# Output projection, second residual and second norm moved within steps 6 and 7 of a fused attention and recurrent kernel

## The reference, cut to what matters

```python
# x: 32 sequences of 256 rows of 128; 16 heads of 64, 4 persistent key/value rows per head
x = x + attention(layernorm(x))          # rms norm, qkv, rope on q and k, causal softmax, output projection
y = layernorm(x)                         # the second norm
# a recurrence over the 32 sequences, on a state c of 256 x 128 (shown for one step):
ft = sigmoid(xt @ wf.T + c @ uf.T + bf)
it = sigmoid(xt @ wi.T + c @ ui.T + bi)
gt = tanh(xt @ wc.T + c @ uc.T + bc)
c = ft * c + it * gt
# at the end
h = tanh(einsum('tbi,oi->tbo', y, wo) + c_final @ uo.T + bo)
x = x + h
```

## Time and profile before

| | |
|---|---|
| median of 3 runs | 1160.55 us (1159.35 to 1161.35) |
| the profiled execution, whole | 1162.89 us |
| its span in the trace | 1161.0 us |
| PE busy with matmuls | 1088.0 us, 94% of the span |
| PE weight loads | 826.2 us, 71% |
| DVE busy | 951.9 us, 82% |
| ACT busy | 707.2 us, 61% |
| POOL busy | 649.2 us, 56% |
| mean granted clock of PE | 0.976 of full speed |

### The profile page before, as it was taken

How to read it: one execution, slowest core, us unless ns; L and a number is a source line. 1 busy time by engine, 2 the same in 40 slices (tenths; PEclk the granted TensorE clock), 3 DMA queues, 4 the chain that set the end, 5 groups by cost and what they waited for, 6 DMA issues and landing times.

```text
span 1161.0 us, 47269 instructions
## 1 busy us (share of the span) xinstructions
PE 1088.0 (94%) x18411; PEld 826.2 (71%) x18411; DVE 951.9 (82%) x3304; ACT 707.2 (61%) x1603; POOL 649.2 (56%) x828
## 2 busy tenths in 40 slices
PE   4879999999999999999999999999999999999981
PEld 2557777777777777777777777777777777777671
DVE  6678888888878988888888888888888888888646
ACT  3556666666556566656666666666666566666634
POOL 3545555556555555655555565555646555655415
PEclk8799999999999999999999999999999999999995
DMA  6213333332333333233333323333332233333205
GB/s 204 93 71 99 112 112 112 112 112 77 96 110 107 113 112 99 90 98 112 105 112 113 110 86 93 110 112 113 112 112 90 85 108 108 108 107 107 72 2 145
DMA packets 78031, 120.52 MB, mean 104 GB/s; under 512 B 13041, under 2 KB 35954, under 8 KB 77682
## 3 DMA queue, kind: packets, MB, share of 16 engines
q1 hardware_dynamic: 68722, 111.21, 31.3%
q10 hardware_dynamic: 9088, 6.29, 2.0%
HBM read 41.56 MB, written 8.78 MB: 43 GB/s over the span
## 4 chain that ended last, share of the span: by engine, by line
PE 57%; DVE 15%; DMA 14%; SPq 5%; issue 4%; POOL 4%; ACT 2%; DVEq 0%; POOLq 0%; ACTq 0%
PE bank_pv L1081 10%; DMA rope_c<-rope_b 10%; PE bank L974 9%; PE bank_st L1037 7%; PE bank_sum L1118 6%; PE bank_sum L1102 4%; PE bank_sm L1013 4%; DMA linv_scratch<-linv 3%; DVE masked L781 3%; PE bank L996 3%; SPq L298 2%; DVE linv L804 2%; PE bank L993 2%; PE bank L1204 2%; PE bank L1206 2%
## 5 line engine op out<-in xcount | busy, mean ns | idle before, releaser
L396 POOL TENSOR_TENSOR qk<-rope_a,rope_c 128x512 f32<-128x512 f32 x256 | 340.7, 1331 | 304.8 <-DMA rope_c<-rope_b 300.8
L781 DVE CUSTOM_DVE_ANT_0 masked<-bank_sm,mask_q 128x132 bf16<-128x132 f32 (+1 forms) x1024 | 307.6, 356 | 44.2 <-PE bank_sm L1013 43.4
L389 POOL TENSOR_TENSOR prob<-prob 128x264 f32<-128x264 f32 x256 | 212.0, 828 | 157.6 <-ACT prob L535 150.7
L535 ACT ACTIVATE prob<-bank_st 128x784 f32<-128x784 f32 x256 | 210.3, 822 | 115.3 <-PE bank_st L1046 114.3
L770 DVE TENSOR_TENSOR rope_a<-bank,cos 128x512 f32<-128x512 f32 x256 | 174.3, 681 | 102.1 <-PE bank L974 74.6
L520 ACT ACTIVATE qk_h<-qk 128x512 f16<-128x512 f32 x256 | 160.2, 626 | 128.9 <-POOL qk L396 128.6
L1081 PE MATMUL bank_pv<-prob,v_sb 128*64 128x256 f32 (+1 forms) x2048 | 224.7, 340 | 0.6 <-DVE raw L797 0.6
L1037 PE MATMUL bank_st<-qk 64*64 64x196 f32 (+3 forms) x4096 | 185.7, 298 | 0.1
L771 DVE TENSOR_TENSOR rope_b<-bank,sin 128x512 f32<-128x512 f32 x256 | 173.8, 679 | 0.0
L1037 PEld LDWEIGHTS bank_st<-qk 64*64 64x64 f32 x4096 | 167.3, 133 | 9.0 <-issue 0.8
L1081 PEld LDWEIGHTS bank_pv<-prob,v_sb 128*64 128x64 f32 x2048 | 124.3, 136 | 54.3 <-issue 0.8
(11 more groups left out here) (202 smaller groups left out, 1793.7 us busy)
## 6 DMA issues: line engine op xcount, KB each, us to landing
rope_c<-rope_b SPq DMA_DIRECT2D x512, 128.0 KB, 2.1
rinv<-linv_scratch SPq DMA_DIRECT2D x124, 256.0 KB, 4.5
out<-x_sb SPq DMA_DIRECT2D x16, 256.0 KB, 2.5
linv_scratch<-linv SPq DMA_DIRECT2D x62, 64.0 KB, 2.1
x_sb<-x ACTq DMA_DIRECT2D x28, 128.0 KB, 5.3
pre<-w_qkv_t ACTq DMA_DIRECT2D x1, 1024.0 KB, 5.3
v_sb<-pm_v SPq DMA_DIRECT2D x64, 8.0 KB
v_end<-v_end_scratch SPq DMA_DIRECT2D x64, 8.0 KB
```

Of the source, the lines that this page charges most:

```text
L389: G.tensor_tensor(prob_2[:, s % 4, :, :], prob[:, s % 4, :, 0:NT - Q1], prob[:, s % 4, :, C0 + Q1:SCOL], ALU.add).then_inc(S["prob_added"], 1)
L396: G.tensor_tensor(qk[:, s, :].rearrange("p (u n) -> p u n", u=2)[:, :, 0:NT], rope_a[:, (NPAIR * j + s) % 3, :].rearrange("p (u n) -> p u ...
L535: A.activation(prob[:, s % 4, :, :], ps_st[:, :, 0:SCOL], ACT.Exp).then_inc(S["exp_done"], 1)
L781: ins = V.tensor_tensor_reduce(masked[:, e, c0:c0 + n], ps_sm[:, e, c0:c0 + n], mask_q[:, c0:c0 + n], 1.0, LOWEST, ALU.add, ALU.max, top[: ...
```

## The change

Nothing is added or removed. Five calls change places within step 6 or step 7, and `residual` is cut in two:

- PE, steps 5 and 6: `project_out` stands ahead of `values` (in step 5 there are no values, so only step 6 changes).
- DVE, step 6: the addition of `residual` (L822) stands ahead of the maxima of pair 3; its statistics, now `second_stats`, stand behind the maxima and ahead of `end_sum`.
- POOL, step 7: `rstd` stands ahead of the `rope_add` of pair 6.
- ACT, step 7: `second_norm` stands ahead of the exponential of pair 7.

```diff
@@ POOL, body
+                    if c and s == 7:
+                        rstd(j - 2)
                     if s >= 1 and a:
                         rope_add(j, s - 1)
-                    if c and s == 7:
-                        rstd(j - 2)
@@ ACT, body
+                    if s == 7 and c:
+                        second_norm(j - 2)
                     if b:
                         exp(j - 1, s)
-                    if s == 7 and c:
-                        second_norm(j - 2)
@@ DVE, residual
                 V.tensor_tensor(at3(x_sb, cj), ps_sum[:, NT:2 * NT], at3(x_sb, cj), ALU.add).then_inc(S["x1_done"], 1)
+
+            def second_stats(cj):
+
                 dve.wait_ge(S["x1_done"], cj + 1)
@@ DVE, body
+                    if s == 6 and c:
+                        residual(j - 2)
                     if s < 3 and b:
                         maxima(j - 1, s + 5)
...
+                    if s == 6 and c:
+                        second_stats(j - 2)
                     if s == 6 and b:
                         end_sum(j - 1)
-                    if s == 6 and c:
-                        residual(j - 2)
@@ PE, body
+                    if s in (5, 6) and c:
+                        project_out(j - 2, p, 2 * (s - 5))
+                        project_out(j - 2, p, 2 * (s - 5) + 1)
                     if s == 6 and a:
                         values(j, p, 0)
                     if s == 7 and a:
                         values(j, p, 1)
-                    if s in (5, 6) and c:
-                        project_out(j - 2, p, 2 * (s - 5))
-                        project_out(j - 2, p, 2 * (s - 5) + 1)
```

## The result

| | before | after |
|---|---|---|
| median of 5 runs each, us | 1161.35 (1159.35 to 1162.14) | 1148.02 (1145.80 to 1149.99) |
| ratio, with its 95% interval | | 0.9885 (0.9869 to 0.9901) |
| profiled execution, whole, us | 1162.89 | 1149.99 |
| its span, us | 1161.0 | 1148.2 |

What follows compares the result with a forecast made beforehand. PE, busy 94% of the span, was taken as the bound, with only its stalls for h_lo and the second norm to gain. 9.9 - 3.7 + 6.9 + 1.0 = 14.1 us, so 1160.55 - 14.1 = 1146.4; range 1141.2 to 1152.8.

Steps and rivals of the forecast that it cites:

- step 6, both terms together: PE and DVE, step 6: 9.9 us gained from waits for h_lo, less 3.7 us lost before the maxima.
- second norm: POOL, DVE, ACT, step 7: factors ahead of the rope's sum end seven steady-round waits of PE, 6.9 us gained.
- ends of the program: Rounds 31 and 32: 2.0 us back at the norm, less 0.35 for the addition and 0.7 for the exponential: 1 us.
- The values no longer wait for h_lo: PE, step 6: 1.88 us of output projection ahead of the values covers all eleven waits, 9.9 us gained.
- Part of it is lost in front of the maxima: DVE, step 6: of a wait w for h_lo, w - 0.37 stays, now before L1021; 3.7 us lost.
- 3 to 4 us in all: Sign in the changed profile: a few waits of L1021 for the maxima, none over 0.9 us, with this total.
- The addition need not wait, and nothing is lost in good rounds: DVE, step 6: output projection ends before the addition starts; steps without a wait for h_lo lose nothing.
- c_lo and the small operations of POOL: DVE and POOL, step 7: c_lo waits some 0.15 us behind prob_add; the factors' four small operations also contend.
- the rival of the small operations: DVE, step 7: c_lo waits until 2.3 us, maxima come 0.45 us late, 6 us lost, 1152.4; chance 0.09.
- the divisions of step 5: Rival, DVE: they meet POOL's sums every round, not one in three; 25 us over 30 rounds, 1167.8; chance 0.07.
- The late exponential: Rival, ACT, step 7: without earlier factors, pair 7's exponential ends 0.2 us late in 31 rounds, 1162.1; chance 0.03.

Runs made afterwards that it cites:

- The cut spread: Second half of the row sums' spread issued behind the swap of pair 3: on the whole change 1154.11 us (0.9920), without DVE's part 1152.06 us (0.9902).
- the plain writes: Whole change with three of POOL's sums near the division replaced by constant writes, output not the reference's: 1145.85 us, ratio 0.9861.

## Why the prediction was right, point by point

| excess and ends, us | forecast | measured |
|---|---|---|
| step 6, both terms together | 9.9 - 3.7 = 6.2 | 10.2 - 5.6 = 4.6 |
| second norm | 6.9 | 7.1 |
| ends of the program | 1.0 | 1.6 less 0.2 at the start |
| step 5 | 0 | -0.8 |
| step 3 | 0 | 0.6 |
| all (the rows agree with it to 0.1) | 14.1 | 12.8 |

- **The values no longer wait for h_lo**: right. In all profiles with PE's part, h_lo is done before the values start 2.45 us into the step (2.74 in the latest rounds). The divisions that now stand ahead of h_lo for PE cost nothing in step 6 either.
- **Part of it is lost in front of the maxima**: right in place and in form. The forecast was that w - 0.37 stays of a wait w; by the rows of before w is l - 0.30, so that is l - 0.67, and the steps give l - 0.72. The size is too small: 3.7 us forecast, 5.6 measured. I had taken the late rounds of the profile of before as those of after. In its profile DVE is late by more: h_lo later than 1.4 us in five rounds, before in two. With the late rounds of before, l - 0.72 gives 3.2 us. In the second profile of the same kernel it is two rounds, and the excess of step 6 is 3.3 us and not 5.6. So the term that was mis-sized is the sum over late rounds. That the forecast 3.7 lies between the two profiles says little. In no profile is h_lo issued later than 1.62 us into step 6; where DVE is later still, the first matmul of step 6 itself waits for its rotation, and that counts in step 5. The steps 5 and 6 together have 6.5 and 5.7 us, against 3.7 forecast. Nor does it confirm the forecast that the new waits in the profile add up to 3.6 us, where "3 to 4 us in all" was expected: that is idle time, and the 3.7 was worked out from start to start. One of these late rounds also gives the 0.64 us in front of the first matmul of step 6 shown above, which goes into step 5, a wait that I hadn't thought of. Whether the change itself makes DVE late a little more often stays open: of the six other profiles with PE's part and the spread in one piece, one has h_lo later than 1.4 us in no round, three in one and two in three.
- **The second norm**: right to 0.2 us, and its times in the step too (2.34 against 2.35 forecast, the exponential 3.12 against 3.14). But POOL's part alone does it; the parts of DVE and ACT were not needed.
- **The addition need not wait, and nothing is lost in good rounds**: right, 18 of the 27 rounds 4 to 30 take 5.29 to 5.30 us in step 6 (12 before).
- **c_lo and the small operations of POOL**: c_lo was to wait some 0.15 us behind `prob_add`. It waits 0.1 in round 16 (0.48 us against 0.39) and not at all in round 18, where it starts at the same time as the first small operation:

```profile
636.78 0.41 DVE L864 SCALAR_TENSOR_TENSOR c_lo<-c,c_hi 128x256 f16<-128x256 f32 x1
636.79 0.46 POOL L404 TENSOR_TENSOR sx_b<-sx_mv,eps 128x2 f32<-128x2 f32 x1 [0.43 <-DVE sx_mv L704]
```

  Here c_lo, which begins first, takes its 0.41 us, and POOL's operation grows from 0.19 to 0.46. c_lo is never longer than 0.49 us in the rounds 4 to 30, where the rival of the small operations had it wait until 2.3 us into the step, so this rival is refuted in this kernel. The Trainium skill, page "SBUF — State Buffer", section "SBUF: two separate sides", has it that the one which starts first holds the shared ports for its whole instruction and the other is blocked. These two rows agree in who waits for whom. In length, all three meetings fall 0.1 us short of waiting for the other's end and then taking one's own time: POOL's operation here would take 0.40 + 0.19 = 0.59 us and took 0.46; in round 16 `prob_add` was first and had 0.2 us to go, so c_lo would take 0.59 and took 0.48; beside the sum of the rope c_lo would take 0.83 + 0.39 = 1.22 and took 1.12.
- **The ends**: +2.0 in round 32, measured 2.06 (the norm's transposition comes 3.92 us after step 7 of round 31 in place of 5.98); -0.7 behind the exponential, measured 0.70 and shown to be ACT's part; -0.35 in round 31 did not come: its step 6 took 5.35 us before and takes 5.29. From step 7 of round 31 to the end, 1.6 us are gained.
- **The rivals**: the divisions of step 5 were said to meet POOL's sums in one round of three. That was a misreading: in the kernel before the pair already takes 1.83 to 1.84 us in 24 of the rounds 3 to 30, and more in the other four. The change did not lengthen it (1.97 us on average before, 1.90 after). The cut spread brought more such meetings about, above all in step 4, and cost about 5 us, with 25 priced. The late exponential came with ACT's part alone, at 0.3 us a round where 0.2 was priced; the 6.7 us that its sum adds are not 0.2 x 31 = 6.2, and no step of the prediction gives them.

**A version that is faster than the kernel before, and probably than the changed one,** is the change without DVE's part: ratio 0.9840 (0.9820 to 0.9859) where the whole change has 0.9868 (0.9849 to 0.9887) on the same chip, with runs that don't overlap, and 0.9855 (0.9829 to 0.9880) on a second one, where the whole change was not run. The intervals touch; what speaks for it beyond the times is the 0.33 us per late round. Without ACT's part it comes to the same. Which of the three is best, the runs don't settle.

## What to carry to other kernels

Two stalls one behind the other can be one engine's lateness handed on: in the profiles taking one away gave 2.0 us, the other 9.3, both 15.5. So before costing a removed stall as a gain, follow the late engine to the next place where it is waited for. Here, moving the operation that others wait for ahead of one that waits for a DMA was worth 0.81%, and making its inputs earlier nothing that could be told; and on an in-order engine such an instruction goes ahead of work that could run only if its input is there, or it costs in every round. A wait that looks like pure loss may keep two engines apart, so look at what it would meet before removing it.

## What the runs showed that I had not expected

- Letting transfers land earlier made the kernel slower: the 28.7 us of DVE's waits for the swaps fell to 0.6, and the pair of divisions in step 4 went from 1.29 to 2.06 us on average, since POOL's sums moved onto it. The whole got 5.4 us slower without DVE's part, on one chip; with it, the ratio rose by 0.0035 to 0.0052, which is 4 to 6 us.
- Small operations suffer as well as large ones from such a meeting: one of 128x2 elements took 0.46 us beside c_lo, 0.19 alone.
- Two profiles of the same kernel, 0.2% apart in time, differ by 2.3 us in one step's stalls, though over all steps they have 8.6 and 8.5 us: the longest of DVE's waits for the swap was 2.6 us in one and 3.4 in the other, and what step 6 doesn't pay step 5 does. Four profiles with the same order on PE and DVE (the two of the whole change, the one without ACT's part, the one with the plain writes) have 6.5, 5.7, 2.0 and 5.0 us in these two steps. A term that rests on how often a round is late is no better known than that.
